# Row maxima and the values' copies spread evenly, and three whole fp32 units of each head made into split units

## The reference, cut to what matters

```python
# B, T, H, D = 2, 2048, 16, 64
q = rmsnorm((x @ Wq).reshape(B, T, H, D));  k = rmsnorm((x @ Wk)...);  v = (x @ Wv)...
gate = softplus(einsum('bthd,hd->bht', k, u_n) / sqrt(D))
bias = -max(i - j, 0) * omega_eff[h] * gate[b, h, j]       # -inf above the diagonal
attn = softmax(q @ k.T / sqrt(D) + bias)
y = attn @ v
return y @ Wproj
```

## Time and profile before

| | before |
|---|---|
| median of 3 runs | 3267.87 us (3264.66 to 3268.54) |
| the profiled execution | 3262.58 us |
| its span, first to last instruction | 3260.8 us |
| PE, PEld busy | 95%, 74% of the span |
| DVE, ACT, POOL busy | 56%, 56%, 48% |
| attention | to about 2100 us of the span |
| the feed-forward network | the rest |

### The profile page before, as it was taken

One profiled execution on the slowest core, in us unless ns is written; L12 is line 12 of the kernel. 1 busy time (PEld: TensorE's weight loads), 2 busy tenths in 40 slices (PEclk: granted clock), 3 DMA queues, 4 the chain that ended last, 5 costly groups with the idle time before them and its releaser, 6 DMA issues. The chain is left out here.

```text
span 3260.8 us, 46767 instructions
## 1 busy us (share of the span) xinstructions
PE 3085.9 (95%) x15184; PEld 2404.4 (74%) x15184; DVE 1837.6 (56%) x4186; ACT 1839.4 (56%) x3185; POOL 1561.4 (48%) x1359
## 2 busy tenths in 40 slices
PE   4899999999999999999999999989999999999998
PEld 3767767767767677677676776678888888788887
DVE  7676677676666766776766767553333332332323
ACT  1677777777776777777777767743333332322222
POOL 5576676676665766766766666613212220000000
PEclk7999999999999999999999999989999999999999
DMA  2342332432432424324324326244434443121210
GB/s 79 71 107 50 86 79 55 105 70 66 103 83 71 98 50 94 74 59 105 70 66 105 69 65 158 70 123 137 121 91 120 116 116 116 57 78 39 71 47 20
DMA packets 210355, 273.95 MB, mean 84 GB/s; under 512 B 68992, under 2 KB 96768, under 8 KB 209984
## 3 DMA queue, kind: packets, MB, share of 16 engines
q1 hardware_dynamic: 210112, 270.97, 32.1%
HBM read 97.25 MB, written 55.90 MB: 47 GB/s over the span
## 5 line engine op out<-in xcount | busy, mean ns | idle before, releaser
L501 POOL TENSOR_TENSOR e_lo<-e_all,e_hi 128x512 fp32r<-128x512 f32 (+1 forms) x832 | 1032.6, 1249 | 612.5 <-ACT e_all L792 526.6
L792 ACT ACTIVATE e_all<-ps_s,bias 128x512 f32<-128x512 f32 (+3 forms) x1280 | 785.3, 624 | 170.7 <-PE ps_s L1134 92.4
L785 ACT ACTIVATE e_hi<-ps_s,bias 128x512 fp32r<-128x512 f32 (+1 forms) x832 | 561.3, 675 | 203.3 <-PE ps_s L1132 125.5
L998 DVE TENSOR_REDUCE maxes<-ps_m 128x1 f32<-128x512 f32 x768 | 516.2, 685 | 225.0 <-PE ps_m L1112 222.7
L1112 PE MATMUL ps_m<-k_ext,q_max 128*128 128x512 f32 (+3 forms) x1280 | 456.2, 379 | 57.7 <-DVE maxes L995 19.5
L1131 PE MATMUL ps_s<-q_twice,k_split 128*128 128x512 f32 (+3 forms) x1280 | 484.3, 378 | 21.3 <-ACT e_all L792 19.8
L1132 PE MATMUL ps_s<-q_ext,k_ext 128*128 128x512 f32 (+3 forms) x1280 | 469.0, 366 | 0.0
L1173 PE MATMUL ps_v<-e_lo,v_both 128*65 128x512 f32 (+1 forms) x832 | 431.4, 519 | 21.0 <-POOL e_lo L501 21.0
L1112 PEld LDWEIGHTS ps_m<-k_ext,q_max 128*128 128x128 f32 x1280 | 243.0, 190 | 219.8 <-DVE maxes L995 58.9
L995 DVE CUSTOM_DVE_ANT_0 ps_m<-ps_m,mask_row 128x128 f32<-128x128 f32 (+3 forms) x512 | 252.7, 495 | 231.0 <-PE ps_m L1112 229.3
L1152 PE MATMUL ps_v<-e_all,v_full 128*65 128x512 f32 (+2 forms) x896 | 324.0, 443 | 0.0
(11 more groups left out here) (234 smaller groups left out, 6566.9 us busy)
## 6 DMA issues: line engine op xcount, KB each, us to landing
q_twice<-q_max SPq DMA_DIRECT2D x256, 128.0 KB, 2.3
yt<-y_out SPq DMA_DIRECT2D x128, 130.0 KB
k_ext<-kq_hi SPq DMA_DIRECT2D x128, 128.0 KB, 2.3
q_max<-kq_hi SPq DMA_DIRECT2D x128, 128.0 KB, 2.4
k_split<-kq_hi SPq DMA_DIRECT2D x128, 128.0 KB, 2.4
k_split<-kq_lo SPq DMA_DIRECT2D x128, 128.0 KB, 2.4
q_ext<-kq_lo SPq DMA_DIRECT2D x128, 128.0 KB, 2.4
hidden<-gelu SPq DMA_DIRECT2D x64, 256.0 KB, 2.1
```

The source lines that it names most:

```text
L501: on.tensor_tensor(e_lo[:, i % LO_RING, off:QB], e_all[:, u_ % E_RING, off:QB], e_hi[:, i % HI_RING, off:QB].bitcast(F32), ALU.subtract).t ...
L785: nc.scalar.activation(e_hi[:, i % HI_RING, off:QB], ps_s[u_ % 2][:, off:QB], ACT.Exp, bias=by).then_inc(hi_done, 1)
L792: nc.scalar.activation(e_all[:, u_ % E_RING, off:QB], ps_s[u_ % 2][:, off:QB], ACT.Exp, bias=by).then_inc(ex_done, 1)
L998: nc.vector.tensor_reduce(maxes[:, qt, kc:kc + 1], ps_m[m % 2][:, 0:width], AX.X, ALU.max).then_inc(mx_free, 1)
```

## The change

Three edits of the step list and of two rules, nothing else:

- `mode_of`: off the diagonal only `kt == 4*qb - 1` stays whole. Of the six whole units off the diagonal three become split: key tile 3 of block 2, key tiles 3 and 7 of block 3. `merged` is widened so that these three have one merged product and VectorE's sum of the 64th column.
- "values in": for the even head due at t0-0.75 to t0-0.19 in steps of 0.14 (before: t0-0.70 to t0-0.54 in steps of 0.04); for the odd head from t0+0.10 in steps of 0.036 (before: from t0+0.05 in steps of 0.04).
- "max": the even head's 40 maxima end at t0+0.44 (before t0+0.24), the odd head's run from t0+0.48 to t0+1.44 (before t0+0.27 to t0+1.08); the special rule for head 1 is dropped.

```diff
-    return "F" if kt < TQ * qb and kt % TQ == TQ - 1 else "P"
+    return "F" if kt == TQ * qb - 1 else "P"
...
-    return kt < TQ * qb and kt % 2 == 0
+    return kt < TQ * qb and (kt % 2 == 0 or MODES[v] != "F" and kt % TQ == TQ - 1)
...
-                at((t0 - 0.70 if s == 0 else t0 + 0.05) + 0.04 * i, "values in", n, i)
+                at(t0 - 0.75 + 0.14 * i if s == 0 else t0 + 0.10 + 0.036 * i, "values in", n, i)
...
-            start, end = (turns[0] + 0.13, t0 + 0.24) if s == 0 else (t0 + 0.27, t0 + 1.08)
+            start, end = (turns[0] + 0.13, t0 + 0.44) if s == 0 else (t0 + 0.48, t0 + 1.44)
...
-                if n == 1:
-                    when = max(0.48 + 0.60 * v / (NM - 1), turns[qb] + 0.13)
```

## The result

The changed kernel takes 3350.03 us (median of 4 runs, 3348.31 to 3351.24) against 3268.20 for the kernel before (4 runs beside them, 3264.66 to 3271.28): a ratio of 1.025, 95% interval 1.0233 to 1.0268. It is 82 us slower where a gain of 13 was forecast, and outside the range.

A forecast was written before the change was run, and what follows sets the result against it. PE bounds S2 and S3, VectorE's chain S4 and S5, POOL S6 into S1. Terms sum to -0.6 us per steady pair, -9 over 15; with first and last pairs about -13, giving 3254 us; 8-in-10 range 3215 to 3302.

The forecast's parts named there:

- S4 and S5: Two consecutive windows of a head pair: added maxima on VectorE's chain lengthen them from 30.84 to 36.0 us, +5.1 a pair.
- The cover for the row of block 3: Odd head, before S6: VectorE's row of maxima ready some 4 us early, so no wait was costed.
- S2: Window of a head pair where PE has no gap: its whole shorter stream shows, -0.63 us a pair, to about 25.0.
- S3: Window of a head pair where PE is the bound: its shorter stream shows fully, -1.66 us a pair, to 26.6.
- S6 and S1: Last window of a pair and start of the next S1: POOL's earlier unit-12 rest gives 38.3 instead of 41.66 us, -3.4.
- PE's full saving: Rival, chance 0.15: VectorE's chain in S4 does not hold PE, a pair gains 2 to 3 us, 3215 to 3235 us.
- POOL is late as well: Rival, chance 0.27: unit 12's rest at S1's start stays late, +1.5 to +2.8 us a pair, 3290 to 3310 us.
- ACT as the bound: Rival, chance 0.05: 96 added exponentials on ACT simply add, up to 66 us, 3334 us.
- the prediction's signs of being wrong: PE waiting little for `maxes` in S4; S6 and S1 near 41.7 us; new `e_lo` waits mid block 3.

## Why the prediction was wrong, point by point

*S4 and S5, +5.1 forecast, +9.0 measured.* The mechanism was right and was seen at each of its points: chain end 20.9 us after S4's start (forecast 21.2), the last maximum at 28.85 (27.7), PE's stream behind it done at about 866.9, 8.5 us later (8.0 and 0.3). The term was 0.9 us too small: 36.85 us for S4 and S5 without other disturbance, against 36.0. The last maximum came later because VectorE had gaps of 0.57, 0.16 and 0.26 us on the way and the bias table took 0.92 us.

*The cover for the row of block 3: this is the step that failed.* The prediction wrote that the row would be ready some 4 us before S6, "if that cover went, block 3 would wait for its row", and costed it at nothing. VectorE's row came 7.5 us before S6's measured start, and about 5.0 before PE was ready, so the cover was there. What was not worked out is SP's queue: the transposed keys had been named as what stood ahead, but not counted, and the loads of weights were not named. When the row is ready, at 861.84, SP has 3.69 us of other issues left (till 865.53) and then 2.55 us of the row's own four: 6.2 us until the last of them is issued, more than those 5. That is 2.4 us a pair, 35 us in all by the kernel with the loads later.

*S2, -0.63 forecast: -0.75 by medians.* Right: PE is the bound there.

*S3, -1.66 forecast: -0.41.* The second step that failed. "Covered by nothing, since PE is the bound there" held for the kernel before. The prediction compared POOL's busy time (22.5 forecast, 21.64 measured) with PE's stream and found it shorter, which it is; but an engine's sum does not tell whether its buffers let it run ahead. With three `e_lo` buffers and a lag of two units POOL waits for PE in the row of split units, and ACT and PE wait in turn. The run with the maxima alone prices it: its S3 takes 27.08 us by medians, the changed kernel's 27.82, so there the units cost 0.7 us where 0.8 was to be saved. S3 with the maxima alone, and the waits in this stretch of the changed kernel:

```profile
798.99:826.08 27.09, 26.96 (x130) 20.80 (x130) 19.36 (x44) 20.01 (x35) 19.81 (x17) 1.00 0.09 21
```

```profile
POOL e_lo L499 <- PE ps_v L1171: 2.8, 3, 1.0
...
ACT e_all L790 <- POOL e_lo L499: 2.0, 3, 1.1
```

*S6 and S1, -3.4 forecast, about -1.4 measured.* The first half came nearly as written: unit 12's rest product starts 23.33 us after S6 (forecast 22.9, before 25.06), still held by POOL, whose idle time before the weights is gone, to be read against the 2.34 us in the earlier trace rows:

```profile
887.83 1.62 POOL L686 TENSOR_TENSOR w_hi<-w_in,one 128x386 fp32r<-128x386 f32 x2 [0.16 <-issue]
```

```profile
892.66 0.45 PE L1171 MATMUL ps_v<-e_lo,v_both 128*65 128x512 f32 x1 [1.83 <-POOL e_lo L499]
...
909.54 0.33 PE L1129 MATMUL ps_s<-q_twice,k_split 128*128 128x128 f32 x1 [1.72 <-ACT e_all L790]
```

The second half did not: from there to S2 (910.28) it took 17.62 us, not 15.4. At the end of S1 PE waits 1.72 us for an exponential that stands on ACT behind the keys' copy into `kq_hi`; ACT was idle for 3.19 us before that copy (907.86). The copy must wait until SP's transfers out of that buffer have landed, and the last of them was issued at 904.49 behind another `shift_rows` and a `q_twice` (899.34 to 903.17). The profile names no releaser there, so that this is SP's queue again is an inference, not shown.

*The rivals.* "PE's full saving" had against it VectorE in S4, rightly. "POOL is late as well" had the right sign (3290 to 3310) by another mechanism. That the maxima would collide with the chain was in the sum; that two further things, SP's order and the ring, would take back what PE's stream gave was in no rival. ACT as the bound (3334 us) falls: the units add all of its exponentials, and by themselves they change the time by 2 us. The rule behind that rival is the Trainium skill's ("Perfetto Trace Analysis", "Identifying the Most-Contended Engine"); the runs here do not bear out the reading that ACT sets the time. Of the prediction's signs of being wrong, two did not come: PE did wait for `maxes` in S4, and S6 and S1 fell to 40.3 us. The third, new waits for `e_lo` in block 3, came on ACT and not on PE (2.0 us, shown above). No sign pointed at SP's queue.

*Summed.* Per steady pair against the forecast: S4 and S5 3.9 more (0.9 VectorE, 2.4 SP, up to 0.7 clock), S2 and S3 1.1 less given, S6 and S1 2.0 less. That is 7.0 us, by 15 pairs 105, where 96 lie between 3254 and 3350. The pair that was read is part of the difference: over all 15 pairs S4 and S5 go from 31.74 to 39.69 us on the mean, +7.95, and a pair grows by 5.6, partly because in four pairs of the kernel before S5 too ran at a lower granted clock (19.5 to 22.2 us). 15 times 5.6 is 84, close to the 82 measured.

## What to carry to other kernels

When steps of a hand-made order are moved, follow the moved step through every queue that it passes, the DMA queue's own issue time included, and count what stands ahead of it there in us; a result that is ready early is no cover if the queue that carries it is full. Work taken off the busiest engine pays only if the buffers let the helpers run ahead: before turning units of one kind into another, count the longest row of equal units against the ring that feeds them. And an order with a serial chain on one engine is best kept free of that engine's other work for as long as the chain lasts; here that gave back 6 us a pair in S4 and S5 against the changed order with the loads later. The 48 us against the kernel before are the whole order's, and mostly not in these stretches.

## What the runs showed of the hardware that was not expected

**PE's clock falls behind waits in S4, in some pairs.** In 9 of the 15 pairs with a chain the granted clock in S4 is lower, and S4 takes 19.7 to 19.9 us in place of 18.2. PE in such a pair:

```profile
842.55 0.50 PE L1110 MATMUL ps_m<-k_ext,q_max 128*128 128x512 f32 x1 [0.89 <-DVE maxes L993]
844.14 0.73 PE L1110 MATMUL ps_m<-k_ext,q_max 128*128 128x512 f32 x1 [1.08 <-DVE maxes L996]
...
845.41 1.91 PE L1150 MATMUL ps_v<-e_all,v_full 128*65 128x512 f32 x2
846.34 1.41 PE L1171 MATMUL ps_v<-e_lo,v_both 128*65 128x512 f32 x1
847.55 0.33 PE L1129 MATMUL ps_s<-q_twice,k_split 128*128 128x256 f32 x1
```

After two waits of about 1 us with one product between them, a whole unit and a rest take from 845.41 to 847.55, 2.14 us, where they took 1.09: the lower level, 1.2 GHz. Most of it is given back in S5 (20.10 against 21.04 us in the windows above), as VectorE worked on meanwhile (18.54 us busy in S4 against 17.04); 0.7 us stays. The other six pairs have the same waits at the same places (the last of 1.08 us, 14.65 us after S4's start, in all 15) and keep 1.00, so what decides between them is not shown. In 5 pairs the clock is lower in S6 behind the wait for the row (21.52 to 21.98 us against 20.38); with the loads later none of these five shows it.

**One transfer costs SP 0.5 to 0.6 us of issue in these rows, the four of a row 2.55 us.** Ten other transfers ahead of a row, 859.73 to 865.53, are 5.8 us.

**A small VectorE step with two operands in SBUF waits for GpSimd.** The bias table (L972, 128 x 64) took 215 to 218 ns in 15 of 32 cases and 631 to 1314 ns in the other 17. Each of these 17 ends 0.1 us after a subtraction of POOL that ran beside it (in the pair above the table 855.10 to 856.02, the subtraction 854.63 to 855.92); none of the 15 has work of POOL beside it. The Trainium skill, "SBUF — State Buffer", "Who interferes with whom", says that a DVE instruction with two SBUF inputs contends with a GpSimd instruction that reads SBUF. The rows agree.
